# Router logits on four column strips with one turn, and one turn of 64 columns for the experts' weights

## What is computed

```python
h = _layernorm(x) * (1 + ca) + sa
x = x + ga * attention(h)            # 16 heads, scores * decay, softmax
h = _layernorm(x) * (1 + cb) + sb
# the expert layer, on xf = h as 2048 tokens of 128 features
shared = silu(xf @ Sg) * (xf @ Su) @ Sd
probs = softmax(xf @ Wr)             # Wr: 128 x 16, the router
topk_p, topk_i = top_k(probs, 2)
cw = zeros(T, 16).at[arange(T)[:, None], topk_i].add(topk_p)
for e in range(16):
    routed += (silu(xf @ Wg[e]) * (xf @ Wu[e]) @ Wd[e]) * cw[:, e]
x = x + gb * (routed + shared)
```

## Time and profile before

| what | value |
| --- | --- |
| median of three runs | 237.63 us |
| the profiled execution's own time | 237.55 us |
| its span, first to last instruction | 235.8 us |
| TensorE busy | 224.9 us of the span |
| VectorE busy | 189.5 us |
| GpSimd busy | 180.6 us |
| ScalarE busy | 164.0 us |
| granted TensorE clock | 1.00 over the whole span |
| DMA engines' mean busy share for the queue that SyncE issues to | 35.7% |

### The profile page before, as it was taken

How to read it: one execution, slowest core, us unless ns; L and a number is a source line. 1 busy time by engine, 2 the same in 40 slices (tenths; PEclk the granted TensorE clock), 3 DMA queues, 4 the chain that set the end, 5 groups by cost and what they waited for, 6 DMA issues and landing times.

```text
span 235.8 us, 5813 instructions
## 1 busy us (share of the span) xinstructions
PE 224.9 (95%) x1824; PEld 166.1 (70%) x1824; DVE 189.5 (80%) x796; ACT 164.0 (70%) x335; POOL 180.6 (77%) x332
## 2 busy tenths in 40 slices
PE   8979899999999999999999999999999999999994
PEld 8676567665666676667676767687788888778882
DVE  3699887998998889899799987387756786956863
ACT  3649667699586999686975796775667659564550
POOL 5779898999897989989999889156477464666551
PEclk9999999999999999999999999999999999999999
DMA  5725836651018711017632640034333420036201
GB/s 150 219 55 130 262 132 144 171 136 45 4 22 200 177 65 36 0 30 197 169 94 90 198 138 0 4 91 134 119 80 121 131 94 0 1 132 200 97 25 44
DMA packets 16622, 24.38 MB, mean 103 GB/s; under 512 B 3344, under 2 KB 6544, under 8 KB 16464
## 3 DMA queue, kind: packets, MB, share of 16 engines
q1 hardware_dynamic: 16160, 24.01, 35.7%
q10 hardware_dynamic: 432, 0.01, 0.1%
HBM read 13.39 MB, written 1.18 MB: 62 GB/s over the span
## 4 chain that ended last, share of the span: by engine, by line
PE 63%; DVE 13%; ACT 11%; SPq 4%; issue 3%; POOL 3%; DMA 1%; DVEq 0%; ACTq 0%
PE bank L967 63%; DVE sc L746 6%; ACT pr L423 4%; SPq L153 4%; POOL sc L306 2%; ACT h_t L365 2%; ACT xn L378 1%; DMA qk_st<-qk 1%; DVE sc L931 1%; DVE qk_st L843 1%; DVE ex L707 1%; DVE mx L746 1%; DVE stats L649 1%; DVE struck L719 1%; ACT L610 1%
## 5 line engine op out<-in xcount | busy, mean ns | idle before, releaser
L306 POOL TENSOR_SCALAR sc<-sc,mx 128x256 f32<-128x256 f32 x256 | 121.3, 492 | 10.6 <-DVE mx L746 9.2
L746 DVE CUSTOM_DVE_ANT_0 sc<-bank,decay 128x256 f32<-128x256 f32 x256 | 91.0, 419 | 11.5 <-PE bank L967 11.3
L423 ACT ACTIVATE pr<-bank 128x512 f32<-128x512 f32 x128 | 69.2, 595 | 17.7 <-PE bank L967 17.7
L967 PE MATMUL bank<-id_f,sc 128*128 128x128 f32 x512 | 69.1, 277 | 3.0 <-ACT pr L423 2.5
L353 POOL TENSOR_TENSOR act_lo<-sc,act_hi 128x512 fp32r<-128x512 f32 x35 | 45.1, 1294 | 34.4 <-ACT act_hi L601 34.4
L967 PEld LDWEIGHTS bank<-id_f,sc 128*128 128x128 f32 x512 | 55.7, 141 | 16.8 <-issue 8.7
L967 PE MATMUL bank<-pr,v_one 128*32 128x256 f32 x512 | 34.3, 385 | 0.0
L925 DVE TENSOR_TENSOR pr<-bank,cwb 128x512 f32<-128x512 f32 x32 | 22.0, 688 | 15.0 <-PE bank L967 14.9
L610 ACT ACTIVATE bank<-bank 128x512 f32<-128x512 f32 x32 | 18.6, 582 | 20.2 <-PE bank L967 19.9
L931 DVE TENSOR_TENSOR sc<-pr,bank 128x512 f32<-128x512 f32 x36 | 24.7, 687 | 6.3 <-ACT bank L610 2.9
L967 PE MATMUL bank<-h_hi,wgu_hi 128*128 128x512 f32 x72 | 28.8, 400 | 0.0
(11 more groups left out here) (117 smaller groups left out, 265.1 us busy)
## 6 DMA issues: line engine op xcount, KB each, us to landing
cwb<-cw_dram SPq DMA_DIRECT2D x64, 128.0 KB, 3.0
qk_st<-qk SPq DMA_DIRECT2D x56, 128.0 KB, 2.7
wgu_sb<-in_w_gu SPq DMA_DIRECT2D x1, 1152.0 KB, 5.8
wgu_sb<-in_x_t SPq DMA_DIRECT2D x4, 256.0 KB, 3.9
x_all<-in_x SPq DMA_DIRECT2D x1, 768.0 KB, 6.6
o_sum<-o_t SPq DMA_DIRECT2D x6, 128.0 KB, 2.2
o_val<-o_t SPq DMA_DIRECT2D x6, 128.0 KB, 2.2
out_dram<-wgu_sb SPq DMA_DIRECT2D x3, 256.0 KB, 3.1
```

Of the source, the lines that this page charges most:

```text
L306: last = nc.gpsimd.tensor_scalar(sc[:, n % RING, t, :], sc[:, n % RING, t, :], -1.0, mx[:, n % RING, t:t + 1], ALU.mult, ALU.add)
L423: nc.scalar.activation(pr[:, n % RING, :, :].rearrange("p a b -> p (a b)"), turn_bank(i, n)[:], ACT.Exp, scale=-1.0).then_inc(s["exp_done" ...
L746: last = nc.vector.tensor_tensor_reduce(sc[:, n % RING, t, :], ps_s[n % SB][:, t * SEQ:t * SEQ + SEQ], decay[:, t, :], float(HD) ** -0.5, ...
L967: return nc.tensor.matmul(o, l, r, start=start, stop=stop, skip_group_check=not check, is_transpose=transpose or None)
```

## The change

The router's product is turned round: the router's weights, padded with zeros from 16 to 32 columns on the host, are now the stationary operand, and h2 of a tile (128 columns) is the moving one. The four tiles' results go to four strips of 32 partitions of one PSUM area. ScalarE copies that area (128 x 128) to SBUF (`logits_out`, r_t), TensorE turns it back in one product (`logits_turn`), and `r_take` reads the 64 columns of interest from a wider area. The experts' weights of a chunk, which lie side by side in cw as 64 columns, are turned by one product in place of four. So cw_t has 64 partitions of 128 columns, and the write to DRAM is four DMAs of 16 rows x 512 bytes in place of one of 16 rows x 2048 bytes. Steps are placed anew on each engine.

```diff
-        wr_sb = sb("wr_sb", [P, E])
+        wr_sb = sb("wr_sb", [P, VW])
+        r_t = sb("r_t", [P, P])
-        cw_t = sb("cw_t", [E, CHUNK])
+        cw_t = sb("cw_t", [TT * E, P])
@@ SyncE
             def weights_out(c):
                 sp.wait_ge(s["cwt_ok"], c + 1)
-                sp.dma_start(cw_dram[c], cw_t[:]).then_inc(s["cw_out"], 16)
+                for t in range(TT):
+                    sp.dma_start(cw_dram[c, :, t * P:t * P + P], cw_t[t * E:t * E + E, :]).then_inc(s["cw_out"], 16)
-                            sp.wait_ge(s["cw_out"], 16 * (c + 2))
+                            sp.wait_ge(s["cw_out"], 16 * TT * (c + 2))
@@ ScalarE
+            def logits_out(c):
+                act_e.wait_ge(s["r_mm"], c + 1)
+                nc.scalar.activation(r_t[:], ps_m[:, 0:P], ACT.Copy).then_inc(s["rt_done"], 1)
+
             def r_take(c):
                 act_e.wait_ge(s["r_done"], c + 1)
-                nc.scalar.activation(lg[:, :, 0:E], ps_m[:, 0:TT * E].rearrange("p (t e) -> p t e", t=TT),
+                nc.scalar.activation(lg[:, :, 0:E], ps_m[:, P:2 * P].rearrange("p (t e) -> p t e", t=TT)[:, :, 0:E],
-                nc.scalar.activation(cw_t[:], ps_m[0:E, :], ACT.Copy).then_inc(s["cwt_ok"], 1)
+                nc.scalar.activation(cw_t[:], ps_m[0:TT * E, 0:P], ACT.Copy).then_inc(s["cwt_ok"], 1)
             def early(i, q):
+                if q == 2 and i > 1:
+                    r_take(i - 2)
             def late(i, q):
                 if q == 1 and i > 1:
-                    r_take(i - 2)
+                    logits_out(i - 2)
                 chunk(i)
+            logits_out(NCHUNK - 2)
             exps(NCHUNK - 1, QUADS - 1, 0)
             r_take(NCHUNK - 2)
                     if i == 1:
-                        if u == 7:
+                        if u == 6:
+                            logits_out(c)
+                        if u == 8:
                             r_take(c)
                     if i == 2:
-                        if u == 1:
+                        if u == 2:
                             router_exp(c)
@@ VectorE
                     if i == 1:
-                        if u == 7:
+                        if u == 8:
                             route_a(c)
-                        if u == 8:
+                    if i == 2:
+                        if u == 0:
                             route_b(c)
-                    if i == 2 and u == 3:
-                        route_c(c)
+                        if u == 3:
+                            route_c(c)
@@ TensorE
             def router(c):
                 pe.wait_ge(s["h2t_ok"], c + 1)
                 for t in range(TT):
-                    last = mm(ps_m[:, t * E:t * E + E], h2_t[:, t * P:t * P + P], wr_sb[:])
-                last.then_inc(s["r_done"], 1)
+                    last = mm(ps_m[VW * t:VW * t + VW, 0:P], wr_sb[:], h2_t[:, t * P:t * P + P])
+                last.then_inc(s["r_mm"], 1)
+
+            def logits_turn(c):
+                pe.wait_ge(s["rt_done"], c + 1)
+                mm(ps_m[:, P:2 * P], r_t[:], id_f[:], transpose=True).then_inc(s["r_done"], 1)
 
             def weights_turn(c):
                 pe.wait_ge(s["cw_ok"], c + 1)
-                for t in range(TT):
-                    last = mm(ps_m[0:E, t * P:t * P + P], cw[:, t, :], id_f[:], transpose=True)
-                last.then_inc(s["cwt_done"], 1)
+                mm(ps_m[0:TT * E, 0:P], cw[:].rearrange("p t e -> p (t e)"), id_f[:],
+                   transpose=True).then_inc(s["cwt_done"], 1)
             def early(i, q):
+                if q == 2 and i > 1:
+                    logits_turn(i - 2)
             turn(NCHUNK - 1, QUADS - 1, 0)
+            logits_turn(NCHUNK - 2)
             values(NCHUNK - 1, QUADS - 2)
                         if u == 6:
                             router(c)
+                        if u == 7:
+                            logits_turn(c)
```

More of the change, by code:

```diff
@@ L131, in build @@
             "at_done at_ok wo_done rt_ok rx_done x2_ok stats2_ok mv2_ok vare2_ok rstd2_ok nmean2_ok nmr2_ok xn2_ok ln2t_done "
-            "h2t_ok h2hi_ok h2lo_ok r_done lg_ok top_ok fill_ok ls_ok struck_ok ex_ok zs_ok rz_ok em_ok "
+            "h2t_ok h2hi_ok h2lo_ok r_mm rt_done r_done lg_ok top_ok fill_ok ls_ok struck_ok ex_ok zs_ok rz_ok em_ok "
             "cw_ok cwt_done cwt_ok cw_out "
@@ L245, in _ @@
             weights_out(0)
-            sp.wait_ge(s["cw_out"], 16)
+            sp.wait_ge(s["cw_out"], 16 * TT)
             for u in range(ROUTED):
@@ L469, in weights_take @@
                 if c:
-                    act_e.wait_ge(s["cw_out"], 16 * c)
-                nc.scalar.activation(cw_t[:], ps_m[0:E, :], ACT.Copy).then_inc(s["cwt_ok"], 1)
+                    act_e.wait_ge(s["cw_out"], 16 * TT * c)
+                nc.scalar.activation(cw_t[:], ps_m[0:TT * E, 0:P], ACT.Copy).then_inc(s["cwt_ok"], 1)
             def split(k):
@@ L1331 @@
         "w_attn": w_attn, "vecs": vecs,
-        "alpha": a["alpha"].reshape(1, 1), "w_r": a["Wr"], "w_gu": w_gu, "w_d": w_d,
+        "alpha": a["alpha"].reshape(1, 1), "w_r": np.pad(a["Wr"], ((0, 0), (0, VW - E))), "w_gu": w_gu, "w_d": w_d,
         "w_mod": a["wmod"].reshape(D, 6, D), "lag": lag, "ident": ident,
```

## The result

| | before | after |
| --- | --- | --- |
| median, 21 executions each | 237.66 us (237.24 to 238.45) | 236.89 us (236.19 to 237.75) |
| the profiled execution's own time | 237.55 us | 237.11 us |
| its span | 235.8 us | 235.2 us |

The ratio is 0.9967, with a 95% interval of 0.9957 to 0.9976: the change makes the kernel 0.77 us faster. Forecast were 236.5 us and a gain of 1.05. The granted clock was 1.00 in both profiled executions. In the changed kernel TensorE's products are L979; VectorE's L694, L732, L738, L746, L925 and L931 are now L705, L743, L749, L757, L936 and L942, ScalarE's L471, L601 and L610 are L477, L610 and L619, GpSimd's L306 and L353 are L308 and L355, and SyncE's L209 and L216 are L211 and L218; in the experiments they differ from these by a line or two.

A forecast was written before the change was run, and what follows sets the result against it. The prediction took TensorE to bound the kernel, without a break in the expert stage and with other engines taking turns in attention. From 237.55 us, gains of 1.91 and a new wait of 0.9 gave 236.5 us, range 235.4 to 237.9.

The forecast's parts named there:

- What bounds the kernel: TensorE, unbroken in the expert stage, where a microsecond less of products is a microsecond less in the end.
- What the blocks cost: On TensorE: attention router 0.30 us from 0.92, expert-stage router 0.52 from 0.90, weights turn 0.15 from 0.43.
- The price near the columns: New attention router taken as 0.30 us, between 0.25 by moving columns and 0.50 by instructions.
- Chunk 0's two places: Attention: chunk 0's router gains 0.07 us (0 to 0.5), its weights turn 0.33 (0 to 0.6).
- Chunk 1's router: Attention: TensorE frees 0.62 us, but VectorE's low half of h2 isn't free, so 0.25 gained (0 to 0.62).
- What comes back as a wait: Expert stage: TensorE waits about 1.0 us for chunk 3's weights where it waited 0.16, a loss of 0.9.
- The covers: Expert stage: late weights covered by 2.0 us; VectorE's units (2, 4) to (2, 6) ready some tenths early.
- the attention stage gives nothing back: Rival: engines beside TensorE take all of chunk 0's and 1's gain, 237.2 us; 16%.
- No new wait: Rival: `route_c` falls between GpSimd's instructions, or the table loads find a gap, 235.5 us; 17%.
- the strips one after the other: Rival: the router's strips don't overlap, so it costs 0.9 us plus the turn, 238.0 at most; 4%.
- the slower case: Rival: chunk 3's weights wait a whole unit longer, or the last weights come over 2.0 us late, 238.6; 13%.
- The sum: Whole kernel: 237.55 us less 1.91 of gains plus 0.9 of wait gives 236.54, said as 236.5.

The follow-up runs named there:

- the run in one place: Changed kernel with the router's four products written to the same 32 partitions, side by side, in place of four strips: 238.53 us, ratio 1.0025.
- the pair with the kernel before: VectorE's low half of chunk 1's h2 moved from round 1 to round 5 in both kernels: changed kernel 236.07 us, kernel before 237.90 us.
- gpsimd_held_back: Changed kernel with GpSimd's lower half of unit (2, 2) held until chunk 3's weights are ready: 235.70 us, ratio 0.9913.
- the first two experiments: Changed kernel with chunk 3's routing steps back in their old units, 236.06 us; changed kernel with GpSimd held until chunk 3's weights are ready, 235.70 us.

## Why the prediction was right, and where it wasn't

- **What bounds the kernel**: right. From chunk 2's router on, every shorter block of TensorE reached the end at its own size (0.57, 0.28, 0.23, 0.31 us for 0.50, 0.28, 0.20, 0.28).
- **What the blocks cost**: right. The router 0.33 us for 0.30 forecast (0.22, if the values are left at their 1.00), in the expert stage 0.57 for 0.52, a turn of 64 columns 0.12 for 0.15. The price near the columns was the right end of the bounds, and the run in one place shows why: the strips work at the same time, be it in their products or in their loads. Leaving the stream of whole-array products costs the strips something: 0.57 against 0.33 in attention. The Trainium skill (TensorEngine Tiling (Array Packing), Key Properties) says that a change of mode drains TensorE; the trace fits that, but no run here separates it from the chain between two products.
- **Chunk 0's two places**: forecast 0.40, measured 0.47 (0.50 with the other reading of the start).
- **Chunk 1's router**: the failed term. The prediction said that VectorE's low half "may start earlier by some 0.58 in all, so 0.25 here". It did start earlier, by 0.47 (119.63 less 0.25, against 119.85), but that is the gain of chunk 0's two places and nothing more: in VectorE's stream the low half stands behind scores that TensorE made ahead of the router, so a shorter router can't move its start. Then it stood for a fourth GpSimd instruction, and the place gave -0.16; the term was 0.4 too large. The 1.95 us were read as a duration, though 1.2 of them were waiting, and the row of chunk 3's weights had led to the right reading: a small VectorE instruction that ends when GpSimd lets it. Its own duration is 0.69. This is shown by the run that moved it, and by the pair with the kernel before. Whether it stands for three or four instructions changes with the same code, and what decides it isn't shown: in the trace of gpsimd_held_back it was three, and the place gave 0.23 (127.38 - 117.19 = 10.19 us from the place before to this one, where it took 127.82 - 117.40 = 10.42), nearly the forecast's number, for another reason.
- **What comes back as a wait**: right in mechanism and size, 0.98 us for 1.0. Silu of (2, 3) stood at 198.88, which is the forecast's 200.0 less the 1.13 that TensorE had gained in that trace by then. Both VectorE products end just behind a GpSimd instruction, and the first two experiments switch the wait off by either of its two causes.
- **The covers**: the prediction called the weights' late arrival covered with 2.0 us in hand, and VectorE's units (2, 4) to (2, 6) "ready some tenths early". In the changed kernel neither cost anything, and both margins had the right size: VectorE ended unit (2, 4) 0.34 us ahead of TensorE's need (204.00 and 204.34), and unit (3, 0) 1.89 ahead (212.95 and 214.84). With the turn a unit later both were used up, and TensorE waited 0.85 and again about 0.3 us.
- **The rivals**: that the attention stage gives nothing back was partly true, at one place of two. No new wait, the strips one after the other and the slower case are excluded by the rows above.
- **The sum**: the forecast was 0.39 us too fast, and that it was no more is in part luck. The terms together were 0.14 too large (1.01 for 0.87), since the others' small misses the other way (0.10, 0.07, 0.03, 0.08, 0.03, less 0.03 and 0.01) made up for two thirds of chunk 1's 0.41; 0.10 lies between the trace's 0.87 and the medians' 0.77, 0.11 between the profiled execution's 237.55 and the median of 237.66, and 0.04 is rounding.

## What to carry to other kernels

A shorter block on the bounding engine pays at its full size only where the engine next in the chain is free at that moment. So ask when that engine is free, what sets that moment, and how much of the length of the instruction it is in is waiting. Before two traces are compared position by position, take off what they differ by ahead of the change: here up to 0.3 us between the two, and 1 us over all twelve. When a line of small steps is moved by a unit, look at the step that stays: it sets the wait; and moving it too may pass the wait on, here to a product and to a DMA, at a loss of 0.55 us. A small SBUF-to-SBUF instruction of VectorE that others wait for belongs outside an unbroken run of GpSimd, or GpSimd is made to wait for it; here each of these gave about as much as the whole change, and one part of two of the change did so alone.

## What the runs showed of the hardware

- VectorE's instruction of 128 x 512 with two inputs in SBUF took 0.69 us alone, and 1.95 to 2.44 us in the eight traces in which it stood beside GpSimd's instructions of 0.47 us that followed each other without a break. It wasn't let in behind the one that was running: it stood until the end of the third (three traces) or fourth (five) and then took 0.73 or 0.74. GpSimd's instruction beside that last part took 1.00 to 1.03 in place of 0.47, and its 30 instructions together 0.59 us longer.
- Two instructions of 0.19 and 0.23 us, with two inputs in SBUF, took 0.95 and 1.20 beside GpSimd's of 1.26 us. The two with one input just ahead of them, beside the same GpSimd instruction, took their usual 0.21 and 0.18.
- Eight instructions of 128 columns took 0.33 us on four strips and 0.96 on one: a factor of 2.9.
- Between whole-array products a turn of 64 columns cost TensorE 0.12 us, and four turns of 16 columns 0.43, so 0.11 each.
- A wait of 0.98 us by its row cost 1.15 us from start to start, and one of 0.16 cost 0.33.
